# A layer norm's inverse square root moved from VectorE to GpSimd, and GpSimd's weight additions placed behind VectorE's scalings

## The chip, the core and the metric

The kernel runs on one core of one Trainium2 chip. The core has five engines with one instruction queue each: PE (TensorE, matrix products into PSUM), DVE (VectorE), ACT (ScalarE), POOL (GpSimd) and SP (SyncE, which here only issues DMAs). They work side by side, each in the order of its own program, and wait for each other through semaphores. The metric is the device time of one execution in microseconds. The kernel before takes 5512.81 us, the median of 3 runs (5504.41 to 5517.73).

## The reference, cut to what matters

128 images of 64x64 pixels and 3 channels go through a small vision tower. Its first part, which takes most of the time, is this:

```python
h = layer_norm(x @ fc0_w + fc0_b, ln0_g, ln0_b)            # 32 channels
for i in range(4):
    x1 = spectral_conv(h, w1[i], w2[i])    # rfft2, keep 12x12 modes twice, 32x32 complex weights per mode, irfft2
    x2 = einsum('bchw,oc->bohw', h, conv_w[i]) + conv_b[i]
    h = layer_norm(x1 + x2, ln_g[i], ln_b[i])              # over the 32 channels of a pixel
    if i < 3: h = gelu(h)
h = gelu(h @ fc1_w + fc1_b); h = gelu(h @ fc2_w + fc2_b); h = h @ fc3_w + fc3_b
...
# layer_norm: (x - mean) * rsqrt(var + 1e-5) * g + b
```

A block of attention and a block of eight experts follow on the resulting 64x64 tokens; the change doesn't touch them.

## The kernel before, in words

The first part is a pipeline over "quads" of four images. There are 32 quads and five phases: `stem` (fc0 and the first norm), three phases `layer`, and `head` (the last norm and the three dense layers), so 160 quads n follow each other, and one more drains the pipeline. Every engine runs the same loops (`quads`) and calls its own `body` for each quad. A quad has four slots k = 0 to 3, and a slot has two units (wh = 0 and 1) of 128x512 values. The order of the instructions is written out by hand; the engines meet only at semaphores, whose counts are computed from n, k and wh.

The way of one unit: PE makes y in PSUM (L888 in the stem, L914 and L922 later). ACT writes its squares (`square`, L1172) and copies y to SBUF (`keep_y`, L1176). DVE sums the squares over each pixel's 32 channels (`sums`, L1352); the means are zero because the weights were centred. When the sums of two slots (128x64 values) are there, `rsqrt_half(n, j)` computes 1/sqrt from them in nine small instructions, L1358 to L1374: a first guess by arithmetic on the bits and two Newton-like steps, each waiting for the one before on the semaphore `norm_step`. We call this the chain; j=0 covers slots 0 and 1 and stands behind slot 1, j=1 covers slots 2 and 3 and stands behind slot 3. Then `normed` (L1345) multiplies y by it, two slots after `sums`: in slot k DVE scales slot k-2. So the first scaling behind the chain j=0 is in slot 2, and that behind j=1 in slot 0 of the next quad. PE transposes the scaled unit (`turn_out`, L934), ACT applies gain, bias and gelu (L1188), PE transposes back (L943), ACT copies (L1181).

Beside it run the transforms. `fwd_h` (PE, L959) at slots 0 and 2 is followed by a transpose on DVE, `turn_w` (L1333), which in the layers stands right behind the two scalings of slots 0 and 2. `inv_w` (PE, L899) at slots 1 and 3 writes the same PSUM bank and so waits for `turn_w`; DVE's `turn_z` (L1327) takes its result, and PE's products for the slots after need that. `fwd_w` (PE, L972) and `turn_modes` (DVE, L1339) end the forward transform, and POOL's `order_x` (L826) brings the modes into order for a store.

What else a quad does depends on its number q in the phase. In q = 8 to 23 ("slot quads", 16 in each of the first four phases) the spectral weights of the next mixing are prepared: POOL loads raw weights by eight DMAs (`load_raw`, L783), ACT brings signs on them (`sign_w1`, L1207, `sign_w2`, L1214), POOL adds a reversed half (`add_weights`, L794), twice a quad. In q = 24 to 31 and in q = 0 to 7 of the next phase ("part quads") a quarter of the modes of eight quads is mixed: PE multiplies (L998) at slots 1 and 3, DVE's `mix` (L1386 and L1388) takes the result into `y_st`, POOL stores `y_st` by four DMAs (`store_part`, L817), and in half of these quads loads modes by six DMAs first (`load_part`, L809). There is one `y_st`: at slot 1 `mix` first waits until the store of the part before has landed (`ymodes_stored`). The layers hold 48 slot quads and 48 part quads.

Of the kernel before, what the change touches and what calls it, by code (L numbers as in the profile page):

```python
# [18 lines left out]
NEWTON = 9  # L19
# [7 lines left out]
def vit_tower(nc, x, p, cst, out, scratch):  # L27
# [5 lines left out]
    with ctx:  # L33
# [25 lines left out]
        var, nt = carve(64), carve(64)  # L59
# [707 lines left out]
        def _(pool):  # L767
# [22 lines left out]
            def add_weights(l, rnd, slot, second):  # L790
                o0, done = rnd * OCH % CH, l * ROUNDS + rnd
                then(pool, "w_scaled", 3 * done + 2 + second)
                view, rev = weight_views(slot, slice(o0, o0 + OCH))
                nc.gpsimd.tensor_tensor(view, view, rev, ALU.add).then_inc(s["w_added"], 1)  # L794
# [25 lines left out]

            def order_x(m):
# [7 lines left out]
            def body(n, q, front, back1, back2, nxt, ph, part=None, chunk=None, seq=None, mixed=0, slots=None):  # L829
# [5 lines left out]
                if slots is not None:  # L835
                    load_raw(ph, q - 8, slots)
                    if q >= 16:
                        load_first(ph, (q - 16) // 4, q % 4)
                if back2 in STORED:
                    order_x(n - 2)  # L840
                if slots is not None:
                    for second in range(2):
                        add_weights(ph, q - 8, slots[second], second)

# [451 lines left out]
        def _(dve):  # L1296
# [57 lines left out]
            def rsqrt_half(n, j):  # L1354

                step, at, r, t, v = s["norm_step"], NEWTON * (2 * n + j), rstd[:, j, :], nt[:, :], var[:, :]
                dve.wait_ge(s["ss_done"], 8 * n + 4 * j + 4)
                v_.tensor_scalar(v, ss[:, j, :], 64.0 / 9.0 / CH, 64.0 / 9.0 * EPS, ALU.mult, ALU.add).then_inc(step, 1)  # L1358
                dve.wait_ge(step, at + 1)
                v_.tensor_scalar(r.bitcast(i32), v.bitcast(i32), -0.5, float(0x5F3759DF), ALU.mult, ALU.add).then_inc(step, 1)  # L1360
                dve.wait_ge(step, at + 2)
                v_.tensor_tensor(t, r, r, ALU.mult).then_inc(step, 1)
                dve.wait_ge(step, at + 3)
                v_.tensor_tensor(t, t, v, ALU.mult).then_inc(step, 1)
                dve.wait_ge(step, at + 4)
                v_.scalar_tensor_tensor(t, t, -10.0 / 3.0, t, ALU.add, ALU.mult).then_inc(step, 1)
                dve.wait_ge(step, at + 5)
                v_.scalar_tensor_tensor(r, t, 5.0, r, ALU.add, ALU.mult).then_inc(step, 1)
                dve.wait_ge(step, at + 6)
                v_.tensor_tensor(t, r, r, ALU.mult).then_inc(step, 1)  # L1370
# [207 lines left out]
```

## Time and profile before

| | |
|---|---|
| median of 3 runs | 5512.81 us |
| the profiled execution | 5508.32 us, its span 5506.6 us |
| granted TensorE clock, mean | 0.961 of full speed |
| busy PE / DVE / ACT / POOL | 91% / 71% / 70% / 16% of the span |
| stem | about 0 to 790 us |
| the three layers | about 790 to 3200 us, some 24.4 us a quad |
| head | about 3200 to 4780 us |
| attention and experts | 4780 to 5506 us |

A span is the time from the first instruction to the last. Busy shares are means over stages that differ: in the layers all of PE, DVE and ACT are busy for most of a quad, in the head PE alone. What counts is which engine's wait ends last at each point of a quad, so the rows below are mostly from the timeline of two quads of a layer: one slot quad (2001 to 2026 us) and one part quad (2243 to 2268 us).

### The profile page before, as it was taken

Reading aid. Unit: us, or ns where it says so; the run is one execution under the profiler, and the core shown is the slowest. Engines: PE = TensorE matmul, PEld = TensorE weight load, DVE = VectorE, ACT = ScalarE, POOL = GpSimd, SP = SyncE. Lnnn points to the kernel's source line nnn. Section 1 sums busy time; section 2 is a strip of 40 time slices with the busy share of each in tenths; the row PEclk is TensorE's granted clock in tenths of the full one; section 3 lists DMA queues with packets and bytes.
Section 4 is the critical chain, followed back from the end, with each engine's and each line's share of the span. In section 5 each row is a group of like instructions: output and inputs, shape, how many; then the busy total and the mean of one; then the engine's idle time right before and its main releaser. Section 6 shows DMA issues by size and latency. Waiting matters only on the chain.

```text
span 5506.6 us, 134680 instructions
## 1 busy us (share of the span) xinstructions
PE 5007.4 (91%) x43556; PEld 2894.5 (53%) x43556; DVE 3901.0 (71%) x7702; ACT 3872.3 (70%) x6261; POOL 901.5 (16%) x1359
## 2 busy tenths in 40 slices
PE   5888889999999999999999999999999999768777
PEld 2444457666767666777666744433333333334333
DVE  4877889888989888999888955545545545444454
ACT  5888877888767888777888766677777777523333
POOL 0133221333121343212333110000000000000000
PEclk9988999999999999999999999999999999878888
DMA  1334467667776676777676732311111111000000
GB/s 62 135 131 140 152 196 238 231 223 237 240 235 230 226 232 229 241 249 236 220 234 227 250 109 72 71 51 49 54 49 51 52 47 53 14 4 4 8 8 4
DMA packets 222593, 756.32 MB, mean 137 GB/s; under 512 B 74033, under 2 KB 113202, under 8 KB 156730
## 3 DMA queue, kind: packets, MB, share of 16 engines
q1 hardware_dynamic: 175162, 632.45, 33.5%
q0 software_dynamic: 47104, 119.60, 8.8%
q8 instruction: 194, 3.18, 0.2%
q14 instruction: 133, 1.09, 0.1%
HBM read 397.49 MB, written 354.42 MB: 137 GB/s over the span
## 4 chain that ended last, share of the span: by engine, by line
PE 58%; DVE 15%; ACT 13%; issue 10%; DMA 1%; ACTq 1%; SPq 1%; DVEq 1%; POOL 0%; POOLq 0%
PE ps_t L1028 8%; PE ps_y L922 8%; PE ps_t L934 5%; PE ps_f L922 4%; PE ps_f L1013 4%; PE ps_y L914 4%; PE ps_t L943 3%; ACT big L1172 3%; DVE big L1345 3%; ACT big L1188 3%; PE ps_t L1037 2%; DVE big L1333 2%; PE ps_s L899 2%; PE ps_y L998 2%; ACT big L1181 2%
## 5 line engine op out<-in xcount | busy, mean ns | idle before, releaser
L1352 DVE TENSOR_REDUCE big<-big 128x16 f32<-128x512 f32 x1280 | 843.7, 672 | 607.8 <-ACT big L1172 604.8
L1345 DVE TENSOR_TENSOR big<-big 128x512 f32<-128x512 f32 x1280 | 937.5, 763 | 33.7 <-DVE big L1374 18.8
L1172 ACT ACTIVATE big<-ps_y 128x512 f32<-128x512 f32 x892 | 545.8, 612 | 469.4 <-PE ps_y L922 415.5
L1188 ACT ACTIVATE big<-ps_t,g_now 128x512 f32<-128x512 f32 x1024 | 818.3, 799 | 15.1 <-PE ps_t L934 14.8
L934 PE MATMUL ps_t<-ident,big 128*128 128x128 f32 x5120 | 800.7, 280 | 29.7 <-DVE big L1345 26.5
L922 PEld LDWEIGHTS ps_y<-conv_now,big 128*128 128x128 f32 x5088 | 616.9, 191 | 362.8 <-issue 362.8
L1181 ACT ACTIVATE big<-ps_t 128x512 f32<-128x512 f32 x1024 | 629.2, 614 | 170.5 <-PE ps_s L959 105.1
L934 PEld LDWEIGHTS ps_t<-ident,big 128*128 128x128 f32 x5120 | 579.9, 143 | 265.9 <-issue 219.3
L922 PE MATMUL ps_y<-conv_now,big 128*128 128x128 f32 x5088 | 717.5, 284 | 0.0
L943 PE MATMUL ps_t<-ident,big 128*128 128x128 f32 x4096 | 638.7, 279 | 86.5 <-ACT big L1181 82.4
L943 PEld LDWEIGHTS ps_t<-ident,big 128*128 128x128 f32 x4096 | 473.5, 143 | 235.9 <-issue 136.6
L1028 PE MATMUL ps_t<-big,fc_w 128*64 128x512 f32 x2048 | 553.2, 618 | 4.2 <-issue 3.3
L1176 ACT ACTIVATE big<-ps_y 128x512 f32<-128x512 f32 x892 | 551.7, 618 | 0.0
L922 PEld LDWEIGHTS ps_f<-conv_now,big 128*128 128x128 f32 x3104 | 376.1, 191 | 141.6 <-issue 141.6
L922 PE MATMUL ps_f<-conv_now,big 128*128 128x128 f32 x3104 | 439.8, 285 | 0.0
L1200 ACT ACTIVATE big<-ps_t,fc_b 128x512 f32<-128x512 f32 x512 | 354.9, 693 | 117.8 <-PE ps_t L1028 117.8
L1172 ACT ACTIVATE big<-ps_f 128x512 f32<-128x512 f32 x388 | 234.1, 603 | 282.7 <-PE ps_f L922 282.4
L1394 DVE COPY w_raw<-ps_t 128x512 f32<-128x512 f32 x256 | 177.1, 692 | 232.8 <-PE ps_t L934 232.8
L1195 ACT ACTIVATE big<-ps_f,fc_b 128x1024 f32<-128x1024 f32 x256 | 287.0, 1121 | 62.4 <-PE ps_s L1019 62.1
L826 POOL COPY x_out<-fw_sb 128x312 f32<-128x312 f32 x256 | 107.2, 450 | 1351.2 <-DVE fw_sb L1339 1351.2
L794 POOL TENSOR_TENSOR wslot<-wslot,w_raw 128x576 f32<-128x576 f32 x128 | 244.4, 1909 | 393.2 <-ACT w_raw L1214 393.1
L817 POOL DMA_DIRECT2D ymodes<-y_st x256 | 154.7, 626 | 861.4 <-DVE y_st L1388 858.4
(197 smaller groups left out, 7625.2 us busy)
## 6 DMA issues: line engine op xcount, KB each, us to landing
hstore<-big SPq DMA_DIRECT2D x256, 1024.0 KB, 4.0
big<-hstore SPq DMA_DIRECT2D x256, 1024.0 KB, 5.3
xmodes<-x_out SPq DMA_DIRECT2D x128, 312.0 KB, 4.4
y_kt<-ymodes SPq DMA_DIRECT2D x512, 78.0 KB
ymodes<-y_st POOLq DMA_DIRECT2D x192, 144.0 KB, 5.7
ymodes<-y_st POOLq DMA_DIRECT2D x64, 192.0 KB, 5.4
mix_room<-xmodes POOLq DMA_DIRECT2D x32, 336.0 KB, 7.1
mix_room<-xmodes POOLq DMA_DIRECT2D x64, 168.0 KB, 9.0
```

What stands on the lines that cost most here:

```text
L922: last = mm(y_of(k % 2, both)[:, wh, 128 * b:128 * b + 128], h_in[k // 2][:, at:at + 128], conv_now[:, :], start=False, stop=(b == 3))
L934: last = nc.tensor.transpose(ps_t1[:, 128 * b:128 * b + 128], y_sb[2 * k + wh][:, 128 * b:128 * b + 128], ident[:, :])
L943: last = nc.tensor.transpose(ps_t2[:, 128 * b:128 * b + 128], h_new[k // 2][:, at:at + 128], ident[:, :])
L1028: last = mm(ps_t2[64 * i:64 * i + 64, :], fc2_w[:, :], gelu1[2 * pr + i], start=True, stop=True)
L1172: af(y_sq[wh], of[:, wh, :], ACT.Square).then_inc(s["sq_done"], 1)
L1176: af(y_sb[2 * k + wh], of[:, wh, :], ACT.Copy).then_inc(s["y_read"], 1)
L1181: af(h_px[2 * (k % 2) + wh], ps_t2[:, :], ACT.Copy).then_inc(s["px_done"], 1)
L1188: af(h_new[k // 2][:, at:at + 512], ps_t1[:, :], ACT.Identity if kind == "stem" else ACT.Gelu, bias=g_now[:, 1:2], scale=g_now[:, 0:1]).th ...
L1195: af(h_new[0][:, 1024 * half:1024 * half + 1024], src, ACT.Gelu, bias=fc1_b[:, :]).then_inc(s["g1_done"], 1)
L1200: af(gelu2[2 * wh + pr], ps_t2[:, :], ACT.Gelu, bias=fc2_b[:, :]).then_inc(s["g2_done"], 1)
L1345: v_.tensor_tensor(groups(y_sb[2 * k + wh]), groups(y_sb[2 * k + wh]), rstd[:, k // 2, at:at + 16].unsqueeze(2).to_broadcast([128, 16, 32] ...
L1352: v_.tensor_reduce(ss[:, k // 2, at:at + 16], groups(y_sq[wh]), AX.X, ALU.add).then_inc(s["ss_done"], 1)
```

## The change

`rsqrt_half` is now a function of POOL's program. GpSimd gets no instruction of the form (a op scalar) op b, so the nine become twelve: five `tensor_scalar` and seven `tensor_tensor` on 128x64 values, each waiting for its predecessor on `norm_step`. DVE's program loses the nine; `normed` waits for `norm_step` as before, now with 12 a chain. In POOL's `body` the chain j=0 stands behind `order_x` in the layers and the head (ahead of it in the stem), and the chain j=1 behind `add_weights` and ahead of `store_part`, and so also ahead of the `load_raw` or `load_part` of the next quad. `add_weights` waits in addition until DVE has scaled slot 0 (first addition) or slot 1 (second) of the quad.

```diff
-NEWTON = 9
+NEWTON = 12
...
-            def add_weights(l, rnd, slot, second):
+            def add_weights(n, l, rnd, slot, second):
+
                 o0, done = rnd * OCH % CH, l * ROUNDS + rnd
+                then(pool, "xhat_done", 8 * n + 2 + 2 * second)
                 then(pool, "w_scaled", 3 * done + 2 + second)
...
+            def rsqrt_half(n, j):
+
+                g_, step, at, r, t, u, v = nc.gpsimd, s["norm_step"], NEWTON * (2 * n + j), rstd[:, j, :], nt[:, :], nu[:, :], var[:, :]
+                then(pool, "ss_done", 8 * n + 4 * j + 4)
+                g_.tensor_scalar(v, ss[:, j, :], 64.0 / 9.0 / CH, 64.0 / 9.0 * EPS, ALU.mult, ALU.add).then_inc(step, 1)
+                then(pool, "norm_step", at + 1)
+                g_.tensor_scalar(r.bitcast(i32), v.bitcast(i32), -0.5, float(0x5F3759DF), ALU.mult, ALU.add).then_inc(step, 1)
+                pool.wait_ge(step, at + 2)
+                g_.tensor_tensor(t, r, r, ALU.mult).then_inc(step, 1)
...
+                then(pool, "norm_step", at + 10)
+                g_.tensor_scalar(t, t, -4.5 / 64.0, 1.5, ALU.mult, ALU.add).then_inc(step, 1)
+                pool.wait_ge(step, at + 11)
+                g_.tensor_tensor(r, t, r, ALU.mult).then_inc(step, 1)
...
+                if front == "stem":
+                    rsqrt_half(n, 0)
                 if back2 in STORED:
                     order_x(n - 2)
+                if front in MIXED:
+                    rsqrt_half(n, 0)
                 if slots is not None:
                     for second in range(2):
-                        add_weights(ph, q - 8, slots[second], second)
-
+                        add_weights(n, ph, q - 8, slots[second], second)
+                if front is not None:
+                    rsqrt_half(n, 1)
                 if part is not None:
                     store_part(part, seq, chunk)
...
-            def rsqrt_half(n, j):
-
-                step, at, r, t, v = s["norm_step"], NEWTON * (2 * n + j), rstd[:, j, :], nt[:, :], var[:, :]
-                dve.wait_ge(s["ss_done"], 8 * n + 4 * j + 4)
-                v_.tensor_scalar(v, ss[:, j, :], 64.0 / 9.0 / CH, 64.0 / 9.0 * EPS, ALU.mult, ALU.add).then_inc(step, 1)
...
-                v_.scalar_tensor_tensor(r, t, 1.5, r, ALU.add, ALU.mult).then_inc(step, 1)
...
-                    if k % 2 and front is not None:
-                        rsqrt_half(n, k // 2)
...
-                    if k == 0:
-                        rsqrt_half(n - 1, 1)
-                    if k == 2 and front is not None:
-                        rsqrt_half(n, 0)
```

First place: DVE in a layer, the end of slot 3 and the begin of the next quad. `big` is the large work buffer, whose first 128x16 outputs are the sums. Before:

```order
L1352 TENSOR_REDUCE big<-big 128x16 [waits sq_done]
L1357 REGISTER_ALU
L1358 TENSOR_SCALAR big<-big 128x64 [waits ss_done]
L1359 REGISTER_ALU
L1360 TENSOR_SCALAR big<-big 128x64 [waits norm_step]
L1361 REGISTER_ALU
L1362 TENSOR_TENSOR big<-big 128x64 [waits norm_step]
L1363 REGISTER_ALU
L1364 TENSOR_TENSOR big<-big 128x64 [waits norm_step]
```

And now, the sums, then the first scaling and what follows it up to the transpose of `turn_w` (here at slot 2 of a quad; slot 0 reads alike):

```order
L1387 TENSOR_REDUCE big<-big 128x16 [waits sq_done]
L1378 ISA [waits y_read]
L1380 TENSOR_TENSOR big<-big 128x512 [waits norm_step]
L1380 TENSOR_TENSOR big<-big 128x512 [waits norm_step,y_read]
L141 REGISTER_ALU
L1368 STREAM_TRANSPOSE big<-ps_s 128x1024 [waits fw_done,f_done]
```

The nine instructions are gone and nothing stands in their place: the next one on DVE is the scaling that waits for the chain's last step, and the transpose stands behind it.

Second place: POOL in a part quad of a layer, from `order_x` to the store. `x_out` and `fw_sb` hold the modes, `ymodes` is in DRAM. Before:

```order
L826 COPY x_out<-fw_sb 128x312 [waits fw_read]
L826 COPY x_out<-fw_sb 128x312
L141 REGISTER_ALU
L817 DMA ymodes<-y_st 384x1x96 [waits mix_read]
L817 DMA ymodes<-y_st 384x1x96 x3
```

And now, the end of the chain j=1 and the store:

```order
L844 REGISTER_ALU
L845 TENSOR_TENSOR big<-big 128x64 [waits norm_step]
L141 REGISTER_ALU
L847 TENSOR_SCALAR big<-big 128x64 [waits norm_step]
L848 REGISTER_ALU
L849 TENSOR_TENSOR big<-big 128x64 [waits norm_step]
L141 REGISTER_ALU
L819 DMA ymodes<-y_st 384x1x96 [waits mix_read]
L819 DMA ymodes<-y_st 384x1x96 x3
```

Two chains (24 instructions) now lie between the copies and the store, and the second of them can't begin before the sums of slot 3.

Third place: POOL in a slot quad of a layer, the additions (`wslot`, `w_raw`). Before:

```order
L794 TENSOR_TENSOR wslot<-wslot,w_raw 128x4x144 [waits w_scaled]
L141 REGISTER_ALU
L794 TENSOR_TENSOR wslot<-wslot,w_raw 128x4x144 [waits w_scaled]
L141 ISA
L783 ISA [waits w_added]
L783 DMA w_raw<-in_tok_w1r 32x576
```

And now:

```order
L141 ISA [waits xhat_done]
L796 TENSOR_TENSOR wslot<-wslot,w_raw 128x4x144 [waits w_scaled]
L141 REGISTER_ALU [waits xhat_done]
L796 TENSOR_TENSOR wslot<-wslot,w_raw 128x4x144 [waits w_scaled]
L141 REGISTER_ALU
L827 TENSOR_SCALAR big<-big 128x64 [waits ss_done]
L141 ISA
L829 TENSOR_SCALAR big<-big 128x64 [waits norm_step]
```

Each addition has a wait for DVE's scalings ahead of it, and the chain j=1 comes between the additions and the next quad's loads.

## Rows read from the trace of the kernel before

**Rows 1.** Page, part 1: busy us, share of the span, instructions

```profile
PE 5007.4 (91%) x43556; PEld 2894.5 (53%) x43556; DVE 3901.0 (71%) x7702; ACT 3872.3 (70%) x6261; POOL 901.5 (16%) x1359
```

**Rows 2.** Windows: length, busy us by engine, clock, DMA share; slot, part, head quads

```profile
1840.00:2230.00 390.00, 364.89 (x3616) 259.20 (x3609) 341.17 (x638) 329.40 (x567) 133.65 (x188) 1.00 0.69 228
2230.00:2420.00 190.00, 186.81 (x2245) 136.70 (x2250) 173.71 (x344) 135.25 (x245) 41.87 (x71) 1.00 0.78 247
3300.00:4760.00 1460.00, 1439.33 (x9174) 567.91 (x9172) 750.66 (x1454) 1038.73 (x1425) 18.74 (x31) 1.00 0.18 53
```

**Rows 3.** Groups by line, DVE: the chain's last and its cheapest instruction

```profile
L1374 DVE SCALAR_TENSOR_TENSOR big<-big 128x64 f32<-128x64 f32 x320 | 72.2, 226 | 11.0
L1360 DVE TENSOR_SCALAR big<-big 128x64 int32<-128x64 int32 x320 | 65.2, 204 | 11.0
```

**Rows 4.** Chain that ended last, slot quad, end of its pass through DVE: start, us

```profile
2015.02 1.17 DVE big L1333
2016.23 0.99 PE ps_s L899 x4
```

**Rows 5.** Timeline, DVE, slot quad: start, us, instruction, idle before

```profile
2010.42 0.69 DVE L1352 TENSOR_REDUCE big<-big 128x16 f32<-128x512 f32 x1 [0.90 <-ACT big L1172]
...
2013.72 1.30 DVE L1345 TENSOR_TENSOR big<-big 128x512 f32<-128x512 f32 x2 [0.34 <-DVE big L1374]
...
2021.02 1.05 DVE L1339 STREAM_TRANSPOSE fw_sb<-ps_s 128x832 f32<-128x832 f32 x1 [0.76 <-PE ps_s L972]
2022.69 0.69 DVE L1352 TENSOR_REDUCE big<-big 128x16 f32<-128x512 f32 x1 [0.62 <-ACT big L1172]
...
2025.68 2.94 DVE L1345 TENSOR_TENSOR big<-big 128x512 f32<-128x512 f32 x2
```

**Rows 6.** Timeline, POOL, the same slot quad

```profile
2010.32 0.50 POOL L783 DMA_DIRECT2D w_raw<-in_tok_w1i  x1 [0.64 <-POOL wslot L794]
...
2022.20 0.83 POOL L826 COPY x_out<-fw_sb 128x312 f32<-128x312 f32 x2 [6.85 <-DVE fw_sb L1339]
2026.10 1.98 POOL L794 TENSOR_TENSOR wslot<-wslot,w_raw 128x576 f32<-128x576 f32 x1 [3.06 <-ACT w_raw L1214]
```

**Rows 7.** Timelines of a part quad: DVE, then PE, then POOL

```profile
2247.80 1.24 DVE L1333 STREAM_TRANSPOSE big<-ps_s 128x1024 f32<-128x1024 f32 x1
...
2258.97 1.29 DVE L1345 TENSOR_TENSOR big<-big 128x512 f32<-128x512 f32 x2
...
2264.87 0.52 DVE L1386 TENSOR_REDUCE big<-ps_y 128x12 f32<-128x384 f32 x1
...
2249.92 0.97 PE L899 MATMUL ps_s<-y_kt,c_inw 64*128 64x416 f32 x4
...
2254.86 2.43 POOL L817 DMA_DIRECT2D ymodes<-y_st  x4 [10.41 <-DVE y_st L1388]
```

**Rows 8.** Groups by line, POOL: busy us, mean ns, idle before

```profile
L794 POOL TENSOR_TENSOR wslot<-wslot,w_raw 128x576 f32<-128x576 f32 x128 | 244.4, 1909 | 393.2 <-ACT w_raw L1214 393.1
...
L826 POOL COPY x_out<-fw_sb 128x312 f32<-128x312 f32 x256 | 107.2, 450 | 1351.2 <-DVE fw_sb L1339 1351.2
...
L325 POOL MEMSET wslot<- 64x64 f32 x1 | 0.1, 145 | 4.1 <-issue 4.1
```

**Rows 9.** Timeline, POOL, a slot quad of the stem

```profile
532.59 0.50 POOL L783 DMA_DIRECT2D w_raw<-in_tok_w1i  x1 [0.29 <-POOL wslot L794]
```

**Rows 10.** DMA issues: count, KB each, median us from issue to landing

```profile
ymodes<-y_st POOLq DMA_DIRECT2D x192, 144.0 KB, 5.7
...
w_raw<-in_tok_w2r POOLq DMA_DIRECT2D x128, 72.0 KB, 4.2
```

**Rows 11.** Waits, whole span: who for whom, total us, times, longest

```profile
PEld ps_s L899 <- DVE big L1333: 49.2, 127, 1.0
```

**Rows 12.** Timeline, DVE, a part quad of the stem

```profile
651.53 0.69 DVE L1352 TENSOR_REDUCE big<-big 128x16 f32<-128x512 f32 x1 [0.49 <-ACT big L1172]
...
658.23 0.55 DVE L1386 TENSOR_REDUCE big<-ps_f 128x12 f32<-128x384 f32 x1
```

More of the change, by code:

```diff
@@ L58, in vit_tower @@
         ss, rstd = (carve(128).rearrange("p (j n) -> p j n", j=2) for _ in range(2))
-        var, nt = carve(64), carve(64)
+        var, nt, nu = carve(64), carve(64), carve(64)
         t_w = carve(2048).rearrange("p (j n) -> p j n", j=2)
@@ L819, in store_part @@
                                  ).then_inc(s["ymodes_stored"], 16)
+            def rsqrt_half(n, j):
[6 more added lines that the diff above has]
+                g_.tensor_tensor(t, r, r, ALU.mult).then_inc(step, 1)
+                pool.wait_ge(step, at + 3)
+                g_.tensor_tensor(t, t, v, ALU.mult).then_inc(step, 1)
+                then(pool, "norm_step", at + 4)
+                g_.tensor_scalar(u, t, -10.0 / 3.0, None, ALU.add).then_inc(step, 1)
+                pool.wait_ge(step, at + 5)
+                g_.tensor_tensor(t, u, t, ALU.mult).then_inc(step, 1)
+                then(pool, "norm_step", at + 6)
+                g_.tensor_scalar(t, t, 5.0, None, ALU.add).then_inc(step, 1)
+                pool.wait_ge(step, at + 7)
+                g_.tensor_tensor(r, t, r, ALU.mult).then_inc(step, 1)
+                pool.wait_ge(step, at + 8)
+                g_.tensor_tensor(t, r, r, ALU.mult).then_inc(step, 1)
+                pool.wait_ge(step, at + 9)
+                g_.tensor_tensor(t, t, v, ALU.mult).then_inc(step, 1)
+                then(pool, "norm_step", at + 10)
+                g_.tensor_scalar(t, t, -4.5 / 64.0, 1.5, ALU.mult, ALU.add).then_inc(step, 1)
+                pool.wait_ge(step, at + 11)
+                g_.tensor_tensor(r, t, r, ALU.mult).then_inc(step, 1)
             def order_x(m):
@@ L1352, in sums @@
                 v_.tensor_reduce(ss[:, k // 2, at:at + 16], groups(y_sq[wh]), AX.X, ALU.add).then_inc(s["ss_done"], 1)
-            def rsqrt_half(n, j):
-                step, at, r, t, v = s["norm_step"], NEWTON * (2 * n + j), rstd[:, j, :], nt[:, :], var[:, :]
-                dve.wait_ge(s["ss_done"], 8 * n + 4 * j + 4)
-                v_.tensor_scalar(v, ss[:, j, :], 64.0 / 9.0 / CH, 64.0 / 9.0 * EPS, ALU.mult, ALU.add).then_inc(step, 1)
[L1359 to L1370, printed above, removed]
-                dve.wait_ge(step, at + 7)
-                v_.scalar_tensor_tensor(t, t, -4.5 / 64.0, v, ALU.mult, ALU.mult).then_inc(step, 1)
-                dve.wait_ge(step, at + 8)
-                v_.scalar_tensor_tensor(r, t, 1.5, r, ALU.add, ALU.mult).then_inc(step, 1)
             def mix(part, seq, k, count, of):
```

## The prediction, made before the changed kernel was run

> **What bounds the kernel now.** I read the busy shares first: PE 91%, DVE 71% [rows 1]. Freeing DVE of a chain looks tempting, but a share says nothing about order, so I went on to the windows. In the layers PE is busy 364.9 of 390 us in slot quads and 186.8 of 190 us in part quads, in the head 1439 of 1460 us [rows 2]. So the head has nothing for a freer DVE to give, and in the layers some 25 us in 390 are open at most. Then the chain of work that ended last, in a slot quad: it runs from ACT's squares through DVE's sums, the Newton chain, the scalings and the transpose L1333 straight into PE's L899 [rows 4]; DVE's transpose ends at 2016.19 and PE starts at 2016.23. The waits say that this is the rule: PE waited for L1333 ahead of L899 127 times [rows 11], out of 192 meetings in the layers (two in each of 96 quads). So the Newton chain is on the path that sets the end. On DVE it is latency more than work, since the instruction behind it needs its result; what counts is the time from the end of the sums to the start of the scaling, not who is busy in it.
>
> **What the chain costs now.** Seven of the nine instructions take 225 or 226 ns, one 223 and one 204, with 34 ns between two (11.0 us over 320) [rows 3]: 2.0 us busy and 0.3 us of gaps. On the timeline: behind slot 3 the sums end at 2010.42 + 0.69 = 2011.11 and the scaling starts at 2013.72, 2.61 us later; behind slot 1 they end at 2023.38 and it starts at 2025.68, 2.30 us later [rows 5]. I call the first meeting A, the second B.
>
> **What it will cost on POOL.** Nothing like these instructions is in the trace, so I bound them. A `tensor_tensor` on 64 columns: no less than the memset of 64x64, 145 ns, which reads nothing; no more than that plus the strided addition's share, 1909 x 64/576 = 212 ns, so 357 ns [rows 8]. I take 250 ns, the middle. A `tensor_scalar`: from 145 ns to 145 + 450 x 64/312 = 237 ns [rows 8]; I take 160 ns, near the memset, since its operands are plain. Between two of them POOL waits for its own semaphore. Low end: DVE's 34 ns [rows 3]. High end: 0.29 us, which POOL took from the end of its addition to the DMA that waits for it [rows 9]. The nearest row is how fast POOL answers DVE: L1339 ends at 2022.07, the copy starts at 2022.20 [rows 5, 6], 0.13 us, which I take for each of the twelve. Back to DVE I add 0.03 us. With T the time from sums to scaling:
>
> T = 7 x 0.25 + 5 x 0.16 + 12 x 0.13 + 0.03 = 4.14 us; low 12 x 0.145 + 12 x 0.034 + 0.03 = 2.18; high 7 x 0.357 + 5 x 0.237 + 12 x 0.29 + 0.03 = 7.2.
>
> The Trainium skill (GPSIMD Engine Reference, § 3.1) has about 2.6 cycles of 1.2 GHz per element for a two-input instruction, which would be an estimate of 139 ns plus dispatch for 64; the additions here took 1909/576 = 3.3 ns per element, more than its 2.2. By the page, T would be about 4.0 with the same gaps. Its § 4.1 says not to move plain elementwise work off VectorE, and the rows agree in so far as twelve steps replace nine.
>
> So A grows by 4.14 - 2.61 = 1.53 us and B by 4.14 - 2.30 = 1.84 us.
>
> **Slot quads (48 in the layers).** A: +1.53, no cover, PE starts within 0.04 us of DVE [rows 4]. At B the moved additions pay something back. The two scalings take 2.94 us at 2025.68, where POOL's addition runs from 2026.10, and 1.30 us at 2013.72, where none does [rows 5, 6]. The addition now waits for these scalings, so 1.64 us go; B is +0.20. The Trainium skill (SBUF — State Buffer, § Who interferes with whom) states that a DVE instruction with two SBUF inputs contends with a GpSimd one that reads SBUF; the trace agrees, 1.64 us. The additions land in DVE's transposes and sums, which read one operand each. Sum: 1.73 x 48 = 83 us. The eight loads of raw weights now stand behind chain j=1: last issue at 2011.11 + 4.14 + 0.64 + 7 x 0.50 = 2019.4, landed 4.2 us later [rows 6, 10] at 2023.6; ACT wants them right behind the squares whose sums start at 2022.69 [rows 5], so about 2023.0 + 1.5. Hidden, with 0.9 us to spare; gone, it would cost ACT that much 48 times.
>
> **Part quads (48).** A: +1.53. B: DVE's transpose ended at 2249.04 and PE came at 2249.92 [rows 7], so 0.88 us of the 1.84 are covered: +0.96. Together 2.49 x 48 = 120 us.
>
> Then a new wait. `store_part` stood behind the mixing of slot 3; now it stands behind chain j=1. After the chain's end: 0.30 us to the first DMA [rows 9], 3 x 0.61 = 1.84 us to the fourth's issue [rows 7], 5.7 us to its landing [rows 10], so 7.84 us. DVE needs y_st free at L1386, which came 2264.87 - 2258.97 = 5.90 us after the scaling's start [rows 7], 5.93 after the chain's end. It will stand 1.91 us. Behind L1386 on DVE are the second half of the mixing, the sums of slot 1, L1339 and again the sums, all without idle before B, so it comes out at B in full. 15 of 16 part quads in a row have a store before them: 45 x 1.91 = 86 us. Before, the last of the DMAs was issued at 2256.7 and landed at 2262.4, 2.5 us early; that was the cover.
>
> **Stem and head.** In the stem's part quads `mix` is the first thing in slot 1. The sums end at 652.22 [rows 12]; the store lands 4.14 + 7.84 later at 664.2 instead of in time for 658.23: 6.0 us, of which I take about 1 as covered by DVE's idle time there, 5 x 7 = 35 us. In the stem's other quads DVE has one or two transposes to do ahead of the waiting scaling and loses little; 0. In the head a slot lasts over 11 us and a chain has a slot to spare: 0, since PE is full [rows 2].
>
> **Sum.** 83 + 120 + 86 + 35 = 324 us on the profiled execution's 5508.3 gives 5832; the median of the runs shown is 4.5 us above that, so 5837 us. With T open the terms are 48 (T - 2.61 + T - 3.94) + 48 (T - 2.61 + T - 3.18) + 86 + 7 (T + 0.83), that is some 199 us for each us of T, zero at T = 2.52.
>
> **Rivals.**
> (a) POOL's steps are short and the freed scalings win. The place is B in slot quads, the price 1.64 us there, and it decides if T is under 2.52 us. At the low end of 2.18 the formula gives 5513 - 199 x 0.34 = 5445 us. For it: the 64x64 memset's 145 ns [rows 8]. Against: it would need 0.03 us between dependent steps, where POOL shows 0.13 and 0.29 [rows 6, 9].
> (b) The store's stall does not come, because the DMAs land in under 3.8 us or DVE is late anyway: 5837 - 86 - 35 = 5716. For it: the landing scatters. Against: the median of 192 is 5.7 us [rows 10].
> (c) POOL takes 0.29 us from each of its own instructions to the next that depends on it, as in [rows 9]: T = 4.14 + 12 x 0.16 = 6.06, 5513 + 199 x 3.54 = 6217 us. Against: that row's wait precedes a DMA.
> (d) The change does what it says for DVE, but DVE isn't what binds, and other slack takes the growth: about 5513 us. Against: L899's waits [rows 4, 11].
>
> **How the numbers follow.** Forecast 0.66, own range 5690 to 6020 (T from 3.4 to 5.0; the granted clock, 1.00 now [rows 2], may also sink while PE waits more); (a) 0.06, (b) 0.14, (c) 0.11, (d) 0.03. The range from 5640 to 6090 takes in (b) and part of the way to (c), and leaves out (a), (d) and most of (c), some 0.2. What can be told from no change is 0.2%, 11 us. Faster by more: (a) less its edge, 0.05; within: the rest of (a) and part of (d), 0.03; slower 0.92.
>
> **What would show it.** On the timeline of the changed kernel: twelve POOL instructions with starts about 0.34 us apart on average and 4.1 us from the sums' end to the scaling at A and B; the scalings at B 1.3 us long in slot quads; L899 waiting over 1 us for the transpose; in part quads DVE idle about 1.9 us ahead of L1386, put down to the DMA ymodes<-y_st; a period of about 26.1 us in slot quads (24.4 now) and about 28 in part quads; head and attention unchanged. DVE's busy time falls by 641 us, and by some 100 us more for the freed scalings. Wrong would be: a T under 2.5 us (then faster), no idle time ahead of L1386 (then b), or L899 not waiting longer than now (then d).

## The result, and the profile after

The changed kernel takes 6091.23 us (median of 4 runs, 6088.1 to 6096.25), beside 5508.78 us for the kernel before on the same chip: a ratio of 1.1056, 95% interval 1.1043 to 1.107, or 582 us more. The forecast was 5837 us with a range to 6090, and the measured median lies just above it. The sign and the place were right; the growth was taken at 324 us instead of 582.

The first part of the page, to be read against [rows 1]:

```profile
PE 5171.0 (85%) x43556; PEld 2973.2 (49%) x43556; DVE 3193.7 (52%) x4822; ACT 3897.1 (64%) x6261; POOL 2096.0 (34%) x5199
```

DVE lost 707 us of work (I had said 641 and some 100), POOL gained 1195, and the kernel grew. PE's busy time grew by 164 us with the same instructions, which is a first hint of a lower clock: over the layers it fell from 1.00 to 0.96.

The timeline of DVE in a slot quad, the answer to [rows 5]:

```profile
2107.19 0.69 DVE L1387 TENSOR_REDUCE big<-big 128x16 f32<-128x512 f32 x1 [0.61 <-ACT big L1207]
2112.94 1.29 DVE L1380 TENSOR_TENSOR big<-big 128x512 f32<-128x512 f32 x2 [5.07 <-POOL big L849]
2114.16 1.24 DVE L1368 STREAM_TRANSPOSE big<-ps_s 128x1024 f32<-128x1024 f32 x1
...
2120.39 0.69 DVE L1387 TENSOR_REDUCE big<-big 128x16 f32<-128x512 f32 x1 [0.90 <-ACT big L1207]
2126.12 1.29 DVE L1380 TENSOR_TENSOR big<-big 128x512 f32<-128x512 f32 x2 [5.05 <-POOL big L849]
```

T, from the end of the sums to the start of the scaling, is 2112.94 - 2107.88 = 5.06 us and 2126.12 - 2121.08 = 5.04 us, where I had forecast 4.14. Both pairs of scalings take 1.29 us, so the 2.94 us pair is gone as forecast. POOL in the same stretch, the chain and what stood behind it (the answer to [rows 6, 9]):

```profile
2121.24 0.24 POOL L827 TENSOR_SCALAR big<-big 128x64 f32<-128x64 f32 x1 [1.33 <-DVE big L1387]
2121.63 0.24 POOL L829 TENSOR_SCALAR big<-big 128x64 int32<-128x64 int32 x1 [0.15 <-POOL big L827]
2121.96 0.29 POOL L831 TENSOR_TENSOR big<-big 128x64 f32<-128x64 f32 x1
2122.33 0.32 POOL L833 TENSOR_TENSOR big<-big 128x64 f32<-128x64 f32 x1
2122.81 0.37 POOL L835 TENSOR_SCALAR big<-big 128x64 f32<-128x64 f32 x1 [0.16 <-POOL big L833]
...
2125.77 0.32 POOL L849 TENSOR_TENSOR big<-big 128x64 f32<-128x64 f32 x1
2126.50 0.56 POOL L783 DMA_DIRECT2D w_raw<-in_tok_w1r  x1 [0.41 <-issue]
```

By line, over the whole span, with busy us, mean ns of one, and the idle time before; this is what [rows 3, 8] had to stand in for:

```profile
L835 POOL TENSOR_SCALAR big<-big 128x64 f32<-128x64 f32 x320 | 138.3, 432 | 42.0 <-POOL big L833 30.1
L839 POOL TENSOR_SCALAR big<-big 128x64 f32<-128x64 f32 x320 | 117.8, 368 | 41.4 <-POOL big L837 29.4
L841 POOL TENSOR_TENSOR big<-big 128x64 f32<-128x64 f32 x320 | 102.5, 320 | 26.7
L831 POOL TENSOR_TENSOR big<-big 128x64 f32<-128x64 f32 x320 | 93.6, 292 | 26.9 <-POOL big L829 0.3
L829 POOL TENSOR_SCALAR big<-big 128x64 int32<-128x64 int32 x320 | 77.8, 243 | 39.8 <-POOL big L827 28.5
```

The mean of L835 is raised by some long ones outside the layers: its median is 377 ns, and in the layers its mean is 379.

The waits, with total, times and longest:

```profile
DVE big L1380 <- POOL big L849: 1035.7, 226, 5.9
...
PE ps_s L934 <- DVE big L1368: 212.6, 193, 1.2
PEld ps_s L934 <- DVE big L1368: 210.2, 159, 1.3
```

The weight load's 49.2 us in 127 waits of [rows 11] became 210.2 in 159. The matrix product itself waited this long before:

```profile
PE ps_s L899 <- DVE big L1333: 19.1, 87, 0.6
```

That became 212.6 in 193, practically every meeting in the layers, 1.1 us each. PE waits for the scaling as well (`turn_out`, L969, 217.3 us after 26.5). As a number for each kind of quad I use the period, the mean distance between two `turn_modes`, of which DVE has one per quad:

| mean period, us | before | after | growth |
|---|---|---|---|
| layers, slot quads (48) | 24.32 | 28.17 | 3.85 |
| layers, part quads (45 of 48) | 25.00 | 31.57 | 6.57 |
| stem, early quads (5 of about 7) | 21.16 | 24.31 | 3.15 |
| stem, slot quads (15 of 16) | 24.25 | 25.16 | 0.91 |
| stem, part quads (7 of 8) | 23.61 | 27.71 | 4.10 |

The means leave out a few quads at the seams of the phases; with all 48 the part quads have 25.08 and 31.60. Taken times 48, 48, 7, 16 and 8, the growths make 185 + 315 + 22 + 15 + 33 = 570 of the 582 us. The head is unchanged: PE is busy 1450.67 of 1480 us in a window of it, as full as in [rows 2] (columns as there):

```profile
1251.04:1278.90 27.86, 22.99 (x217) 15.91 (x218) 15.51 (x21) 21.28 (x36) 15.86 (x36) 1.00 0.57 195
1306.76:1335.37 28.61, 24.57 (x217) 17.44 (x218) 15.62 (x21) 21.14 (x36) 15.88 (x36) 0.94 0.55 190
1335.37:1365.33 29.96, 25.92 (x217) 17.75 (x218) 15.62 (x21) 21.79 (x37) 16.68 (x37) 0.89 0.59 192
...
3880.00:5360.00 1480.00, 1450.67 (x9214) 570.19 (x9206) 650.01 (x930) 1046.08 (x1435) 252.05 (x739) 1.00 0.17 52
```

The first three windows are single slot quads. The same 217 PE instructions take 27.86 us of wall time in the quad whose granted clock is 1.00 (2.4 GHz throughout) and 29.96 us in one at 0.89 (part of it at 1.2 GHz). Before, the layers stood at 1.00 throughout; after, they average 0.96.

### The profile page after: what moved, and what is told of

Read it like the earlier page. It is cut to its first block, busy times and chain, and to the rows that moved or that the text cites. A ratio compares the mean times of both kernels' runs of the same rounds, so it can differ in the third digit from the quotient of the medians.

```text
span 6086.2 us, 136684 instructions
## 1 busy us (share of the span) xinstructions
PE 5171.0 (85%) x43556; PEld 2973.2 (49%) x43556; DVE 3193.7 (52%) x4822; ACT 3897.1 (64%) x6261; POOL 2096.0 (34%) x5199
## 4 chain that ended last, share of the span: by engine, by line
PE 33%; DVE 7%; issue 5%; POOL 5%; ACT 4%; DMA 2%; DVEq 0%; ACTq 0%; POOLq 0%; SPq 0%
PE ps_t L1063 7%; PE ps_y L957 5%; PE ps_f L1048 3%; PE ps_y L949 2%; PE ps_t L1072 2%; PE ps_t L969 2%; DMA ymodes<-y_st 2%; PE ps_f L957 1%; PE ps_t L352 1%; ACT big L1230 1%; DVE big L1368 1%; PE ps_f L342 1%; PE ps_f L934 1%; ACT big L1207 1%; DVE big L1387 1%
## 5 line engine op out<-in xcount | busy, mean ns | idle before, releaser
L1380 DVE TENSOR_TENSOR big<-big 128x512 f32<-128x512 f32 x1280 | 856.1, 700 | 1178.5 <-POOL big L849 1035.7
L969 PE MATMUL ps_t<-ident,big 128*128 128x128 f32 x5120 | 825.1, 285 | 220.8 <-DVE big L1380 217.3
L1207 ACT ACTIVATE big<-ps_y 128x512 f32<-128x512 f32 x892 | 538.7, 604 | 494.6 <-PE ps_y L957 422.4
L1223 ACT ACTIVATE big<-ps_t,g_now 128x512 f32<-128x512 f32 x1024 | 804.7, 786 | 78.6 <-PE ps_t L969 74.3
L969 PEld LDWEIGHTS ps_t<-ident,big 128*128 128x128 f32 x5120 | 592.8, 145 | 489.8 <-DVE big L1380 270.7
L827 POOL TENSOR_SCALAR big<-big 128x64 f32<-128x64 f32 x320 | 77.4, 242 | 2067.8 <-DVE big L1387 2062.7
L978 PE MATMUL ps_t<-ident,big 128*128 128x128 f32 x4096 | 656.5, 285 | 85.0 <-ACT big L1216 82.6
L978 PEld LDWEIGHTS ps_t<-ident,big 128*128 128x128 f32 x4096 | 487.2, 146 | 250.9 <-issue 148.7
L1211 ACT ACTIVATE big<-ps_y 128x512 f32<-128x512 f32 x892 | 544.3, 610 | 0.0
L957 PEld LDWEIGHTS ps_f<-conv_now,big 128*128 128x128 f32 x3104 | 402.8, 203 | 156.0 <-issue 156.0
L957 PE MATMUL ps_f<-conv_now,big 128*128 128x128 f32 x3104 | 468.6, 297 | 0.0
L934 PE MATMUL ps_s<-y_kt,c_inw 64*128 64x416 f32 x780 | 210.2, 617 | 212.6 <-DVE big L1368 212.6
L796 POOL TENSOR_TENSOR wslot<-wslot,w_raw 128x576 f32<-128x576 f32 x128 | 237.3, 1854 | 222.7 <-DVE big L1380 219.7
```

Source lines behind the costliest of these rows:

```text
L957: last = mm(y_of(k % 2, both)[:, wh, 128 * b:128 * b + 128], h_in[k // 2][:, at:at + 128], conv_now[:, :], start=False, stop=(b == 3))
L969: last = nc.tensor.transpose(ps_t1[:, 128 * b:128 * b + 128], y_sb[2 * k + wh][:, 128 * b:128 * b + 128], ident[:, :])
L978: last = nc.tensor.transpose(ps_t2[:, 128 * b:128 * b + 128], h_new[k // 2][:, at:at + 128], ident[:, :])
L1207: af(y_sq[wh], of[:, wh, :], ACT.Square).then_inc(s["sq_done"], 1)
L1211: af(y_sb[2 * k + wh], of[:, wh, :], ACT.Copy).then_inc(s["y_read"], 1)
L1223: af(h_new[k // 2][:, at:at + 512], ps_t1[:, :], ACT.Identity if kind == "stem" else ACT.Gelu, bias=g_now[:, 1:2], scale=g_now[:, 0:1]).th ...
```

## The experiments

The ratio is to runs of the kernel before on the same chip. The periods are those of the layers, in us (before: 24.32 and 25.00).

| kernel | us | ratio, 95% interval | slot | part | against after |
|---|---|---|---|---|---|
| after | 6091.2 | 1.1056 (1.1043 to 1.107) | 28.17 | 31.57 | |
| e2, two operations per instruction | 6014.8 | 1.091 (1.0893 to 1.0927) | 27.46 | 31.25 | -76 |
| e4, chain of eight | 5851.9 | 1.0619 (1.0602 to 1.0635) | 25.24 | 30.50 | -239 |
| e8, long chain on DVE | 6125.3 | 1.1113 (1.1096 to 1.113) | 27.90 | 30.12 | +34 |
| e1, store ahead of the chain | 6050.9 | 1.0973 (1.0956 to 1.0989) | 28.21 | 31.34 | -40 |
| e10, store from SP | 6021.3 | 1.0921 (1.0904 to 1.0938) | 28.20 | 30.87 | -70 |
| e9, after with its costs cut | 5751.9 | 1.044 (1.0413 to 1.0467) | 26.61 | 27.30 | -339 |
| e5, the additions' move alone | 5488.0 | 0.9957 (0.9944 to 0.9971) | 24.20 | 25.03 | |
| e6, turn_w between the scalings | 5504.3 | 0.9986 (0.9977 to 0.9995) | 24.21 | 25.00 | |
| e7, e5 with turn_z first | 5447.3 | 0.9883 (0.9868 to 0.9898) | 23.36 | 25.00 | |
| e11, e7 and e6 | 5432.1 | 0.9856 (0.9837 to 0.9875) | 23.14 | 25.00 | |

**e2: what the short instructions cost.** In the trace of after, two of the five `tensor_scalar` lines, those with one operation, are the slow ones.

```
-g_.tensor_scalar(u, t, -10.0 / 3.0, None, ALU.add)
+g_.tensor_scalar(u, t, 1.0, -10.0 / 3.0, ALU.mult, ALU.add)
...
-g_.tensor_scalar(t, t, 5.0, None, ALU.add)
+g_.tensor_scalar(t, t, 1.0, 5.0, ALU.mult, ALU.add)
```

> The changed kernel with the two tensor_scalar of one operation (add -10/3, add 5) written with two (times 1, then the add), same values. In the changed kernel's trace the one-operation ones take 0.37 us and the two-operation ones 0.24. Theory: the form decides, T falls by 0.26 us from 5.04, and at some 199 us per us of T the time falls by about 50 us to 6040. Rival: something else about these two places makes them long (what stands before them): they stay at 0.37 and the time stays at 6091.

Measured 76 us less than after. POOL by line:

```profile
L835 POOL TENSOR_SCALAR big<-big 128x64 f32<-128x64 f32 x320 | 97.1, 304 | 41.9 <-POOL big L833 30.0
...
L839 POOL TENSOR_SCALAR big<-big 128x64 f32<-128x64 f32 x320 | 78.2, 244 | 41.3 <-POOL big L837 29.4
```

The form with a useless multiplication is the faster one: 244 instead of 368 ns, and 304 instead of 432. DVE's idle time ahead of a scaling fell from 5.05 to 4.82 us. At the prediction's slope of 199 us per us of T the step is worth some 50 us; the mean clock rose too, from 0.944 to 0.953 over the span. That the clock is the source of the rest is argued, not shown. So the form of two instructions was worth about as much as moving the store to another queue (e10, below).

**e4: is T the lever?** The second correction of the inverse root is left out, so the norms are less exact.

```
-NEWTON = 12
+NEWTON = 8
...
 g_.tensor_tensor(r, t, r, ALU.mult)     # L841, now the last
-(the four instructions of L843 to L849 and their waits)
```

> The changed kernel without the last four instructions of the chain (the second correction of 1/sqrt is left out, NEWTON = 8); its output is less exact. Theory (latency of the chain, nothing else): T falls from 5.04 to 3.46 us; at 199 us per us of T that is 314 us less, about 5777. If the slope of the formula is right, slot quads of the layers fall by 2 x 1.58 = 3.2 us each. Rival (the loss comes from what POOL does later: loads, stores, additions behind the chain, or from waits that don't scale with T): a fall by much less, say under 150 us, to over 5940.

T fell to 3.48 us:

```profile
2121.63 0.69 DVE L1379 TENSOR_REDUCE big<-big 128x16 f32<-128x512 f32 x1 [1.25 <-ACT big L1199]
2125.80 1.29 DVE L1372 TENSOR_TENSOR big<-big 128x512 f32<-128x512 f32 x2 [3.49 <-POOL big L841]
```

Slot quads gave 2.93 us back for 2 x 1.56 = 3.12 us of T, nearly one for one (some of it is the clock's, granted at 0.99 in e4's slot quads and 0.97 in after's). Part quads gave only 1.07, so the total is -239 us where 1.56 x 199 = 310 was due. The waits of after and of e4 show most of the difference:

```profile
DVE big L1399 <- DMA ymodes<-y_st: 91.9, 51, 4.8
```

```profile
DVE big L1391 <- DMA ymodes<-y_st: 187.2, 51, 6.8
```

DVE stands at the store instead: 51 waits grew from 91.9 to 187.2 us. That is not because it comes there sooner. Without the wait `mix` would have come 5.7 us behind the store's first issue in both kernels, since both stand behind the chain's end. What changed is the landing:

```profile
ymodes<-y_st POOLq DMA_DIRECT2D x192, 144.0 KB, 6.0
```

The median is 6.0 us after 4.3 in the changed kernel (its line is below), and 1.7 us in each of 51 waits is 87 of the 95 us of growth. Why the same DMAs land later in this kernel no run shows. A store's landing time read in one kernel can't be carried to another.

**e8: POOL, or only the latency?** The kernel before with the additions moved as in e5, nothing of the chain on POOL, and ten copies that depend on each other at the chain's end on DVE.

```
-NEWTON = 9
+NEWTON = 19
...
+for extra in range(10):
+    dve.wait_ge(step, at + 9 + extra)
+    v_.tensor_copy(t, r).then_inc(step, 1)
```

> The kernel before with the additions behind the scalings and the chain on DVE made longer by ten small copies of 128x64 values, each waiting for its predecessor (19 steps instead of 9): nothing of the chain is on POOL, but from the sums to the scaling it takes about 2.3 + 10 x 0.26 = 4.9 us at B and 5.2 at A, as long as on POOL in the changed kernel (5.04). Theory (latency, whichever engine): by the prediction's terms slot quads of the layers 24.3 + 2.6 + 0.96 = 27.9 us as in the changed kernel (28.2), part quads, without the late store, 25.0 + 2.6 + 1.7 = 29.3; the stem loses some 4 to 5 us a quad, since DVE's transposes can't go on beside it; together about 6000 us. Rival (what costs is that POOL has the work: its later stores and loads, its slow issue, contention on SBUF): the time stays under 5650.

```profile
2125.18 0.69 DVE L1353 TENSOR_REDUCE big<-big 128x16 f32<-128x512 f32 x1 [0.67 <-ACT big L1173]
...
2128.22 2.26 DVE L1378 COPY big<-big 128x64 f32<-128x64 f32 x10
2130.52 1.29 DVE L1346 TENSOR_TENSOR big<-big 128x512 f32<-128x512 f32 x2
```

T is 2130.52 - 2125.87 = 4.65 us here and 4.78 at the next meeting. DVE has only the 0.03 us gaps between the steps in it, POOL is free of the chain, and still the slot quads take 27.90 us, near after's 28.17; the T of the two meetings add up to 9.8 us on average over these quads, 9.9 in after. PE waited for `turn_w` 194 times, 205.1 us. So in the layers a chain of this length is enough for the growth, without any of it on POOL: whoever executes it, PE stands still for it. The total is even above after's, since the stem's DVE has no room (its quads took 28.65 to 31.18 us).

**e1 and e10: the store.** In e1 POOL issues the store's four DMAs ahead of chain j=1; in e10 `store_part` stands on SP's queue, at the end of its body.

```
-if front is not None: rsqrt_half(n, 1)
 if part is not None: store_part(part, seq, chunk)
+if front is not None: rsqrt_half(n, 1)      # e1
```

> The changed kernel with POOL's store of y_st put back ahead of the chain j=1, all else as changed. Theory (the path: sums, chain on POOL, scaling, transpose, L899): DVE's wait ahead of L1399 for the DMA, 91.9 us over 51 times in the changed kernel, goes; but the four issues, 2.4 us, now run until about 0.9 us after the sums of slot 3 have ended, so the chain j=1 starts that much later in 48 part quads of the layers, 43 us. Net some 45 us less than 6091, about 6045. Rival 1: the store's wait was covered by other idle time: no gain and the later chain shows, about 6135. Rival 2: the store is all that makes part quads lose more than slot quads (6.6 against 3.7 us each): part quads fall by nearly 3 us, about 5950.

```
-    pool.dma_start(dst[t]..., y_st[...])    # in POOL's body
+    sp.dma_start(dst[t]..., y_st[...])      # e10: in SP's body
```

> The changed kernel with the four DMAs that store y_st issued by SP at the end of its quad instead of by POOL: the store doesn't wait for the chain j=1, and the chain doesn't wait for the store. Theory: DVE's wait for ymodes<-y_st ahead of L1399 goes (91.9 us over 51 times), and chain j=1 starts on time, unlike in the kernel with the store ahead of it (6051): part quads of the layers 1 to 1.5 us shorter, those of the stem 3 us, 6091 - 75 = about 6015. Rival: part quads are long for another reason (the chain starts later in them, TensorE's clock), and only the stem gains: about 6070.

e1 gave 40 us, e10 70 us. In both the stem's part quads became some 3 us shorter (24.69 and 24.43 after 27.71), those of the layers 0.23 and 0.70. Neither kernel has a wait of DVE for the store left. The difference is seen in one of e1's part quads, DVE first and then POOL:

```profile
2679.21 0.69 DVE L1387 TENSOR_REDUCE big<-big 128x16 f32<-128x512 f32 x1 [0.27 <-ACT big L1207]
2686.64 1.29 DVE L1380 TENSOR_TENSOR big<-big 128x512 f32<-128x512 f32 x2 [6.74 <-POOL big L849]
```

```profile
2681.07 0.59 POOL L819 DMA_DIRECT2D ymodes<-y_st  x1 [0.21 <-issue]
2681.74 0.24 POOL L827 TENSOR_SCALAR big<-big 128x64 f32<-128x64 f32 x1
```

The sums ended at 2679.90, but POOL was issuing DMAs until 2681.66, so the chain began 1.84 us behind them and T was 6.74. This is one of the worst quads: in 14 of the 48 the chain j=1 began 0.9 to 1.85 us behind the sums, in the others within 0.2, on average 0.50 (0.14 in after and in e10). In e1 the store and the chain stand in each other's way on one queue; in e10 they don't. The DMAs also land sooner from SP's queue, 2.5 us in the median.

**e5: the other half of the change.** The kernel before with the additions placed behind the scalings, the chain left on DVE.

```
 def add_weights(n, l, rnd, slot, second):
+    then(pool, "xhat_done", 8 * n + 2 + 2 * second)
     then(pool, "w_scaled", 3 * done + 2 + second)
```

> The kernel before, chain on DVE, with only the second part of the change: the additions wait for DVE's scalings. Theory: the two scalings at B shrink from 2.94 to 1.3 us in slot quads, but ACT has no idle time behind B there, so PE's 0.2 us wait is all that comes back in the layers, and 0.7 us a slot quad of the stem: some 20 us less, about 5490. Rival (the credit of 1.64 us at B that the sum gave to each slot quad is there in full with the short chain too): 48 x 1.64 = 79 us less in the layers and some 10 in the stem, about 5420. Rival 2: the additions come later and hold up ACT's second sign pass: slower than 5510.

```profile
2006.35 1.29 DVE L1346 TENSOR_TENSOR big<-big 128x512 f32<-128x512 f32 x2
...
2018.61 1.29 DVE L1346 TENSOR_TENSOR big<-big 128x512 f32<-128x512 f32 x2 [0.32 <-DVE big L1375]
```

The second pair fell from 2.94 us [rows 5] to 1.29, and the kernel became 24 us faster. The Trainium skill (SBUF — State Buffer, § Who interferes with whom) states this contention, and here it is reproduced by moving nothing but the additions. But the layers' slot quads gained only 0.12 us of the 1.65 freed; 1.11 came in each slot quad of the stem (24.25 to 23.14). The rest reappears as idle time of DVE ahead of the sums, where it waits for ACT's squares, 604.8 us before and now:

```profile
DVE big L1353 <- ACT big L1173: 675.9, 490, 3.0
```

What still holds the quad is a wait that the kernel before had too, at the same size: DVE ahead of `turn_modes` for `fwd_w`, and PE ahead of `fwd_w` for `turn_z` (37.9 us in 48 waits before, 37.8 now).

```profile
L1340 DVE STREAM_TRANSPOSE fw_sb<-ps_s 128x832 f32<-128x832 f32 x128 | 133.7, 1045 | 35.3 <-PE ps_s L973 35.3
```

e7 tests it.

**e7, e6 and e11: giving the room away.** In e7 `turn_z` of slot 1 goes ahead of the scalings on top of e5, in e6 `turn_w` goes between the two scalings in the kernel before, and e11 has both. The cuts show where the calls go; they are gone from behind the `wh` loop.

```
+if both and k == 1: turn_z(n, 1, ps_s)               # e7, ahead of the wh loop
 for wh in range(2):
+    if wh and both and k == 0: turn_w(n - 2, 1, ps_s)    # e6
+    if wh and both and k == 2: turn_w(n - 1, 0, ps_s)    # e6
     ... normed(...)
```

> The kernel before with DVE's transpose L1333 (turn_w) of the layers between the two scalings ahead of it instead of behind both: it ends 0.64 us earlier, the second scaling 1.2 us later. Theory 1: L899's wait for that transpose sets the end at A, so 0.6 us come back at A in each of 96 quads, about 5455. Theory 2: DVE is busy without a gap from the chain's end to its transpose L1327, for which PE's L972 waits, and its total there is unchanged: no change, about 5510.

> The kernel before with the additions behind the scalings (5488 alone) and, in slot 1 of the layers' quads, DVE's transpose L1327 (turn_z) ahead of the two scalings of that slot instead of behind them. Theory: PE's L972 stops waiting for L1327 (0.8 us in a slot quad, 48 times, 37.9 us in all in the trace of before), and as DVE's stretch from A to there is on the path in slot quads, about 30 us come back: 5458. Rival: ACT's sign pass follows in that slot and ends later than PE anyway, so under 10 us: about 5485.

> The fastest kernel so far (chain on DVE, additions behind the scalings, turn_z first in slot 1; 5447) with turn_w between the two scalings. Alone that order gave 7 us, when DVE was busy without a gap from the chain to turn_z and its total there was unchanged. Theory: with turn_z now early, L899's time sets when iw comes and so when turn_z and L972 can run; 0.6 us earlier at A and B where PE waits: 20 to 50 us less, about 5410. Rival: ACT or PE are bound by then, no change: 5445.

e6 alone gave 7 us, little more than the noise: a transpose that PE waits for comes 0.6 us sooner, and DVE's work behind it is not sooner for that. PE's wait for `turn_w` is gone and its wait for `turn_z` grew from 37.9 to 48.6 us. e7 gave 64 us, of which e5 explains 24; the wait that e5 had left is gone, and a slot quad takes 23.36 instead of 24.20 us:

```profile
L1340 DVE STREAM_TRANSPOSE fw_sb<-ps_s 128x832 f32<-128x832 f32 x128 | 133.3, 1041 | 0.4 <-PE ps_s L973 0.4
```

e11 has the lowest median of the study, 15 us under e7 and 1.4% under the kernel before, with the chain left where it was; the intervals of e7 and e11 overlap, and the slot quads' 0.22 us times 48 would be 11 us.

**e9: can the chain stay on POOL?** After with e2's forms, e10's store, and the three transposes moved ahead of both scalings, so that DVE does `turn_w` while POOL is in the chain.

```
+if both and k == 0: turn_w(n - 2, 1, ps_s)
+if both and k == 1: turn_z(n, 1, ps_s)
+if both and k == 2: turn_w(n - 1, 0, ps_s)
 for wh in range(2): ...
```

> The chain on POOL as in the changed kernel, with its waiting time filled: two-operation forms (as in the 6015 kernel), y_st stored by SP (as in the 6021 kernel), and in the layers DVE's transposes ahead of the scalings, L1333 (turn_w) in slots 0 and 2 and L1327 (turn_z) in slot 1, so that DVE does turn_w while POOL computes. Theory (only what stands behind the chain on the path counts): PE's L899 then comes after the first scaling and one transpose on PE, T + 1.2 us behind the sums instead of T + 2.5: some 1.5 us less at each of two meetings, 0.26 us less of T, and what the two single experiments gave: slot quads about 24, part quads about 26.5 us, together about 5615 us. Rival 1: the second scaling or ACT takes the transpose's place as the last wait: about 5750. Rival 2: the loss is fixed by T alone wherever the transposes stand: about 5940.

Measured 5752 us: 339 under after and 243 over before. DVE's timeline and PE's say what is left:

```profile
2104.29 0.69 DVE L1387 TENSOR_REDUCE big<-big 128x16 f32<-128x512 f32 x1 [1.45 <-ACT big L1207]
2105.26 1.25 DVE L1368 STREAM_TRANSPOSE big<-ps_s 128x1024 f32<-128x1024 f32 x1 [0.28 <-PE ps_s L994]
2109.77 1.29 DVE L1380 TENSOR_TENSOR big<-big 128x512 f32<-128x512 f32 x2 [3.27 <-POOL big L851]
```

```profile
2110.52 0.66 PE L969 MATMUL ps_t<-ident,big 128*128 128x128 f32 x4 [1.02 <-DVE big L1380]
```

The transpose is covered, the scaling isn't: PE's `turn_out` needs it. And the raw weights, whose loads stand behind the chain on POOL's queue, are late for ACT in this faster kernel, as its waits say:

```profile
ACT wslot L1242 <- DMA w_raw<-in_tok_w2i: 44.1, 32, 2.3
ACT wslot L1242 <- DMA w_raw<-in_tok_w2r: 41.1, 29, 2.2
```

So somewhat more than half of the loss can be taken back, not all of it: by e2 and e10 alone some 146 us of the 339 are the forms and the store, and the rest goes with the transposes. The short chain on DVE stays far ahead. Starting the chain earlier, slot by slot, was not tried.

## Why the prediction was right or wrong

**Right.** What bounds the kernel: the chain is on PE's path, and it is latency, not share, that counts (e8). The loads of raw weights were still nearly covered (ACT waited 9.9 us for them in all; in e9, whose quads are shorter, 85.2); DVE's loss of work (707 us, 641 and some 100 said); the gaps of the chain, in the layers 0.08 us behind a plain wait and 0.16 where the wait is an instruction of its own (medians), about 0.11 on average where I took 0.13; head unchanged; the rivals (a), (b) and (d) dead, (c) dead as a mechanism, though its 6217 us stood nearer to the result than my 5837.

**The step that failed: the durations in T.** "I take 250 ns, the middle" for a `tensor_tensor` and "160 ns, near the memset" for a `tensor_scalar". Measured, the seven `tensor_tensor` take 5 x 320 + 2 x 292 = 2.18 us, where I had 1.75; the five `tensor_scalar` take in the layers 242 + 243 + 377 + 368 + 243 ns = 1.47 us, where I had 0.80. That is 3.65 us for 2.55, and the gaps are 0.2 less: T = 5.04. The bounds held for one kind (145 to 357) and not for the other: 145 to 237 ns, under all five. Its upper end I had made from a strided copy by scaling part of its time with the number of elements; that a fixed cost of the instruction was scaled down with it is argued. Both values were chosen below the truth, on the side of a memset that reads nothing. By the Trainium skill (GPSIMD Engine Reference, § 3.1) the estimate was 139 ns a `tensor_tensor`, and the run shows more than twice that at 64 columns. From 320 ns at 64 columns and the 1854 ns of the 576-column additions in the same trace (L796) I estimate 3.0 ns a column and some 130 ns that don't go with the columns. The prediction's "about 4.0" for T by the page doesn't follow either: 139 ns with its own other terms gives 3.36, and the rest would be a dispatch time for which it names no source.

With T = 5.04 the prediction's own formulas give 169 for the slot quads, 206 for the part quads, 86 and 41: 502 us instead of 324. The mis-sized durations are 178 of the missing 258 us. The rest, term by term:

| term | forecast | at T = 5.04 | measured |
|---|---|---|---|
| slot quads | 83 | 169 | 185 |
| part quads without the store | 120 | 206 | 282 |
| store's wait, layers and stem | 121 | 127 | 60 |
| stem's other growth | 0 | 0 | 43 |

The store's share is e10's: 0.70 x 48 + 3.3 x 8 = 60 us by the periods (70 in the total). Part quads without it are (6.57 - 0.70) x 48. The stem's other growth is 22 + 15 + (4.10 - 3.3) x 8.

**The second failed step, in the part quads: a cover that wasn't there.** I let 0.88 us of B be covered in each, since PE came 0.88 us after DVE in the one quad of [rows 7]. Without that cover the chain costs 2 x 5.04 - 4.91 = 5.17 us in a part quad; measured are 5.87 (without the store's wait). Averaged over the part quads, T is 5.23 and 4.98 at the two meetings after 2.45 and 2.62, a growth of 5.14. In e8 it is 4.72 and 5.02, a growth of 4.7, and measured are 5.12. In both kernels the growth comes through whole and a little more. A gap read at one meeting need not be slack: it may itself come from the chain one quad earlier. That reading is argued, and since the lower clock is in the measured numbers too, how much of the 0.88 us was covered is not shown.

**The store: too large.** 1.91 us a quad was forecast, 0.70 measured. The wait itself was nearly right. In a part quad of the changed kernel `mix` came 7.38 us behind the scaling (which starts at 2678.62) and had waited 1.40, so without the wait it would have come at 5.98, where I had 5.90; over the layers there are 43 waits of 1.45 us. DVE's timeline there, the answer to [rows 7]:

```profile
2686.00 0.56 DVE L1399 TENSOR_REDUCE big<-ps_y 128x12 f32<-128x384 f32 x1 [1.40 <-DMA ymodes<-y_st]
```

The DMAs landed sooner than in [rows 10], 4.3 us in the median instead of 5.7:

```profile
ymodes<-y_st POOLq DMA_DIRECT2D x192, 144.0 KB, 4.3
```

Why is open: e4, also slower than the kernel before, has 6.0. The step that failed is "it comes out at B in full". In e10 DVE's 62.4 us of these waits in the layers' part quads are gone, and 27.5 of them come back there as longer waits for ACT's squares, 9 as longer waits for the chain. Only about half of a wait that is taken away shortens the quad.

**The stem at 0.** I wrote that the transposes ahead of the waiting scaling cover the chain there. They don't: e4, with T at 3.48, brings the early quads to 20.24 us, under before's 21.16, and after has 24.31. The chain is on the path there too.

**The clock, left out of the sum.** It was named only as a widening of the range. In the three slot quads of the windows above, 0.06 of granted clock goes with 0.75 us and 0.11 with 2.1 us of 28; against the quad at 1.00 the mean growth is 0.31 us a quad, some 15 us in 48. But in the third layer a slot quad at 1.00 takes 27.12 us; with each layer's quads held against its own at 1.00 it is 0.56 us a quad, 27 us in 48. In the part quads and the stem I can't separate it. What the engine had done before was to wait for `turn_w`, by 1.1 us at each meeting. e1 shows one PE group at both levels:

```profile
2485.42 0.97 PE L934 MATMUL ps_s<-y_kt,c_inw 64*128 64x416 f32 x4 [1.10 <-DVE big L1368]
...
2498.62 1.76 PE L934 MATMUL ps_s<-y_kt,c_inw 64*128 64x416 f32 x4 [1.10 <-DVE big L1368]
```

**The credit at B.** The 2.94 us pair became 1.29 as forecast. In the changed kernel it counts in full, as the slot term shows (185 us, some 27 of them the clock's, against 169 with the credit and 248 without). But in a kernel with the short chain it counts for little: e5 got 6 us of it in the layers. A saving is worth what the next wait leaves.

**Open.** Why the one-operation `tensor_scalar` is slower; why the third layer's slot quads are 0.74 us shorter than the first's at the same clock of 1.00 (27.12 and 27.86); how the rest of the part quads' growth (0.5 to 0.7 us each) divides between clock and queues.

## What to carry to other kernels

A chain of small dependent instructions is priced by its latency at the point where somebody waits for it: count steps, take the duration of one small instruction and one gap on the engine that will execute it, and ignore the busy shares. Where no such instruction is in the trace, do not scale a large one down by its elements; measure one before moving twelve; here even the upper bound of one kind, 237 ns, was too low. And ask of every saving which wait comes last after it: here moving the additions was worth 24 us, and 64 with one transpose ahead of the scalings, while moving the chain as well, which looked like a load on DVE, made the kernel 582 us slower. And taking a wait away gives back only what nothing else covers: of 1.45 us at the store about half.

## What the runs showed of the hardware

- On GpSimd a `tensor_scalar` of 128x64 float32 with one operation took 368 ns, and with two operations 244 ns (e2, same line, 320 instructions each).
- There a `tensor_tensor` of 128x64 took 320 ns, and 292 ns where both inputs are the same tile (L831). DVE's small instructions of the same size took 204 to 226 [rows 3].
- A wait that is an instruction of its own costs 0.07 us more between two dependent GpSimd instructions than one that the instruction carries: ahead of L839 of the changed kernel 0.16 us in 184 chains that have it, and 0.09 in 136 that don't.
- A GpSimd addition of two 128x576 operands beside a pair of VectorE multiplications made that pair 1.65 us longer (2.94 and 1.29, e5).
- The same store of 144 KB landed 5.7 us after its issue in the kernel before, 4.3 in the changed one and 6.0 in e4, all from GpSimd's queue, and 2.5 from SyncE's (e10); all medians.
